# Attention over stacked halves, weight units split by GpSimd, and trimmed ends in a fused attention and feed-forward kernel

## The chip, the cores and the metric

The kernel runs on one core of a Trainium2 chip. The metric is the device time of one execution in microseconds (us). Engines: TensorE (PE, matmuls; PEld its weight loads), VectorE (DVE), ScalarE (ACT), GpSimd (POOL), and SyncE (SP), which only issues DMAs here.

## The reference

128 batches of 64 rows by 1024 columns go through two residual blocks. `itok` names one of 16 conditions for each batch.

```python
def cond(x, weights, condition):            # 64x64 matrix of the batch's condition, mixes the 64 rows
    return jnp.einsum('bct,bcd->bdt', x, weights[condition])

def attn(x, Wqkv, bqkv, Wo, bo):            # one head, d = 256
    q, k, v = split(jnp.einsum('bsc,cf->bsf', x, Wqkv) + bqkv)
    a = softmax(jnp.einsum('bqd,bkd->bqk', q, k) * scale)
    return jnp.einsum('bqd,dc->bqc', jnp.einsum('bqk,bkd->bqd', a, v), Wo) + bo

def cond2(x, ids, weight):                  # 1024x1024 matrix of the batch's condition
    return jnp.einsum('bsi,boi->bso', x, weight[ids])

# ffn: x W^T + b, and a low-rank product whose rank (8, 16, 32, 64) a gate chooses for each row
x = x + attn(cond(x, cond_weights, itok), ...)
x = x + ffn(cond2(x, itok, cond2_weight), ...)
```

## The kernel before

All is computed with numbers kept as two float16 halves, a high and a low one. A product of two such numbers takes three matmuls: high by high, high by low, low by high (the function `three`).

**Phase A (attention).** 64 steps, each with a pair of batches (`a_step(i, q)`; `i` counts 16 bodies of four steps; two pairs make a group of four batches, which lies in a ring of four in SBUF). The row mix and Wqkv are swapped: z = x Wqkv is formed first, then the 64x64 matrix is applied to q, k and, behind the softmax, to v. In a step stand, in this order on TensorE: eight chunks of z for the next pair (`z_part`, L1179, six matmuls each of 128x384), and between them the links of this pair's chain: q/k products (L1214), scores (L1226), transpose of the probabilities (L1231), u = probabilities by mix (L1236), o = z's v part by u (L1244), and four output products of the group before (`out_products`, six matmuls of 128x256). The two batches of a pair share 128 partitions; the mix of a pair is a 128x128 matrix with two 64x64 blocks and zeros beside them (`wcf`, `wch`, `wcl`).

Each link is evicted by ScalarE (high half: `zh`, `qkh`, `pth`, `uh`, `oh`) and then VectorE (low half: `zl`, `qkl`, `ptl`, `ul`, `ol`). Both also split x for the pair after next (`x_hi`, `x_lo`: xs), the next mix (`mix_hi`, `mix_lo`) and add bias and residual for the output products (`out_chunks`, `residual`).

**Weight units.** The 16 matrices of 1024x1024 for phase B are split meanwhile: 64 units of 128x2048 float32 in two stage buffers. For each step ScalarE makes the high half (`unit_hi`, L670) and VectorE the low one (`unit_lo`, L875) in three pieces, and SP stores it to `ws` in DRAM and loads another (`unit_turn`). Four last units (the W of the feed-forward) are split in the first two steps of phase B and stay in SBUF.

**Phase B (feed-forward).** 64 steps with the batches sorted by condition, so that each of the 16 matrices (and one that straddles two streams) is loaded once, in four parts of 1 MB, by GpSimd's DMA queue (`load_condition`, L602). GpSimd works out the order in the first 41 us and then only issues those loads. TensorE runs condition products (`cond_set`, L1284 and L1286), gate and feed-forward (`ffn_main`, L1315 and L1317).

The order on every engine is written out by hand and each instruction waits on semaphores; there is no scheduler. A DMA queue (SP's, GpSimd's) serves its issues in order.

Of the kernel before, what the change touches and what calls it, by code (L numbers as in the profile page):

```python
# [21 lines left out]
ALU = mybir.AluOpType  # L22
# [21 lines left out]
PIECES = ((0, T), (T, T + T // 2), (T + T // 2, 2 * T))  # L44
NPC = len(PIECES)
# [27 lines left out]
def build(nc, NB, x_in, ids_in, wc_in, wqkv_in, wo_in, w2_in, w_in, ag_in, bl_in, bias_in, gb_in, out, x1, ws):  # L73
# [11 lines left out]
    with ctx:  # L85
# [28 lines left out]
        zh_flat = sb("zh", [P, 2 * NQ], F16)  # L114
        zl_flat = sb("zl", [P, 2 * NQ], F16)
        zh = zh_flat[:, :].rearrange("p (r n) -> p r n", r=2)
        zl = zl_flat[:, :].rearrange("p (r n) -> p r n", r=2)
        qkh = sb("qkh", [P, 4, P], F16)
        qkl = sb("qkl", [P, 4, P], F16)
        wcf = sb("wcf", [P, 4, 2 * P], F32)  # L120
        wch = sb("wch", [P, 2, 2 * P], F16)
        wcl = sb("wcl", [P, 2, 2 * P], F16)
        sm = sb("sm", [P, P], F32)
        ex = sb("ex", [P, P], F32)
        pn = sb("pn", [P, P], F32)
        soft = sb("soft", [P, 4], F32)
        pth = sb("pth", [P, P], F16)
        ptl = sb("ptl", [P, P], F16)
# [5 lines left out]
        tt = zh_flat[:, 0:8 * P].bitcast(F32).rearrange("p (r m n) -> p r m n", r=2, m=2)  # L134
        yf = zl_flat[:, 0:8 * P].bitcast(F32).rearrange("p (r m n) -> p r m n", r=2, m=2)
# [67 lines left out]
        bank = [ctx.enter_context(nc.psum_tensor(f"bank{n}", [P, 512], F32)) for n in range(8)]  # L203
        zps = [[bank[0], bank[1]], [bank[2], bank[3]]]
        qkps, chps, wops = bank[4], bank[5], [bank[6], bank[7]]
# [7 lines left out]
        s_wuh, s_wul = sem("unit_piece_hi"), sem("unit_piece_lo")  # L213
# [47 lines left out]
        s_chunk = [sem(f"chunk{n}_loaded") for n in range(NCH)]  # L261

# [53 lines left out]
        def _(sp):  # L316
# [5 lines left out]
            def load_mix(i, q):  # L322

                n = q % 4

                wait(sp, s_wcl, i, 4, q - 3)
                sp.sem_inc(s_turn_sp, 1)
                for b in range(2):
                    e = sp.value_load(idr_i[0:1, bass.ds(8 * i + 2 * q + b, 1)], min_val=0, max_val=NC - 1)
                    dst = wcf[b * S:(b + 1) * S, n, :].rearrange("p (t d) -> p t d", t=2)[:, :, b * S:(b + 1) * S]  # L330
                    src = wc_in[bass.ds(e, 1), :, :, :].rearrange("a c t d -> (a c) t d")
                    sp.dma_start(dst, src).then_inc(s_wc[n], 16)
# [11 lines left out]

            def load_unit(i, q):

                if isinstance(i, int) and 4 * i + q >= UNITS_A:
                    n = 4 * i + q - UNITS_A
                    src = w_in[:, n * UNIT:(n + 1) * UNIT]
                else:  # L350
                    src = w2_in[bass.ds(i, 1), :, q * UNIT:(q + 1) * UNIT].rearrange("a p n -> (a p) n")
                sp.dma_start(stage[:, q % 2, :], src).then_inc(s_unit[q % 2], 16)

            def store_unit(i, q):

                dst = ws[bass.ds(i, 1), :, q, :, :].rearrange("a p h n -> (a p) h n")
                sp.dma_start(dst, split_w[:, q % 2, :, :]).then_inc(s_us[q % 2], 16)

            def unit_turn(i, q, load=True):

                wait(sp, s_wul, i, 4 * NPC, NPC * (q - 1))
                sp.sem_inc(s_turn_sp, 1)
                if q < 2:
                    store_unit(i - 1, q + 2)
                else:
                    store_unit(i, q - 2)
                if load:
                    load_unit(i, q)
# [16 lines left out]
            sp.dma_start(group_cols(0, PT2, PT2), x_in[0, :, PT2:GR]).then_inc(s_x[0], 16)  # L385
# [4 lines left out]
            for n in range(6, K):  # L390
                load_chunk(n)
            load_mix(0, 1)
            for n in range(2):
                sp.sem_inc(s_us[n], 16)
            load_unit(0, 0)
            load_x(0, 1)
            load_unit(0, 1)
# [5 lines left out]
            def body(i, first=False, last=False):  # L403
                for u in range(2):
# [11 lines left out]
                    here = (i, 2) if u == 0 else (i + 1, 0)  # L416
                    late_units = last and u == 1
                    unit_turn(*here, load=not late_units)
# [4 lines left out]
                    unit_turn(here[0], here[1] + 1, load=not late_units)  # L423
                    if late_units:
                        for q in range(2):
                            load_unit(IA, q)
# [36 lines left out]
            for q in range(2, 4):  # L463
                sp.wait_ge(s_wul, NPC * (UNITS_A + q - 1))
                load_unit(IA, q)

# [18 lines left out]
            store_out(IB - 1, 1)  # L485
            for u in range(2):
                sp.wait_ge(s_out[u], 64 * IB)
# [3 lines left out]
        def _(pool):  # L491
# [93 lines left out]
            PACE = 8  # L585

            def load_condition(n):
# [4 lines left out]
                for u in range(2):  # L592
                    pool.wait_ge(s_us[u], 32 * cond + 48)
                    pool.sem_inc(s_turn_pool, 1)
                for t in range(TS):
                    if n == 0:
                        pool.wait_ge(s_z, PACE * (t + 1))
                    else:
# [7 lines left out]
            def first_slots():  # L606
# [4 lines left out]
                pool.wait_ge(s_z, NP)  # L611
# [10 lines left out]
            pool.wait_ge(s_wl, K + 4)  # L622
            pool.wait_ge(s_order, 1)
# [9 lines left out]
        def _(act):  # L633
# [9 lines left out]
            def mix_hi(i, q):  # L643
                wait(act, s_wc[q % 4], i, 32, 32 * (q // 4 + 1))
# [10 lines left out]
            for n in range(K):  # L655
                chunk_hi(n)
                if n == 5:
                    mix_hi(0, 0)
                if n == 6:
                    x_hi(0, 1)  # L660

# [747 lines left out]
```

## Time and profile before

| what | value |
|---|---|
| median of 3 runs | 2286.02 us (2283.11 to 2287.87) |
| the profiled execution's own time | 2283.59 us |
| its span, first to last instruction | 2281.9 us |
| TensorE busy | 2246.7 us, 98% of the span |
| VectorE, ScalarE, GpSimd busy | 1236.8, 953.2, 61.3 us |
| mean granted TensorE clock | 0.999 of full speed |
| DMA engines, slices in phase A | 0.6 to 0.8 busy, 245 to 303 GB/s |
| weight units loaded / stored | 68 / 64 of 1024 KB, 8.8 / 6.9 us from issue to landing (median) |

Busy time says which engine is full; the chain that ended last says what set the end; the timeline of one stretch says how an instruction stands to its neighbours. Times of matmuls overlap, so their cost in a row is read from start to start.

### The profile page before, as it was taken

To read this page: it belongs to the slowest core of one execution; us is meant where nothing else is said; L and a number is where in the kernel's file an instruction comes from. 1 tells how busy PE (TensorE), PEld (TensorE's weight loads), DVE (VectorE), ACT (ScalarE), POOL (GpSimd) and SP (SyncE) were. 2 spreads that over 40 slices of the span, in tenths; PEclk is the share of its full clock that TensorE was granted. 3 is DMA by queue.
4 is the path that set the end of the run, shared out by engine and by line. 5 is a ranking of instruction groups with operands and counts; after the bars stand their busy time and mean duration, and the time that the engine had idled before them with its cause. 6 is when DMAs were issued, how large, how long until landed. Compare 5 with 4: busy or idle time off the path is not lost.

```text
span 2281.9 us, 73807 instructions
## 1 busy us (share of the span) xinstructions
PE 2246.7 (98%) x28506; PEld 1748.9 (77%) x28506; DVE 1236.8 (54%) x3438; ACT 953.2 (42%) x2461; POOL 61.3 (3%) x128
## 2 busy tenths in 40 slices
PE   7999999999999889999999999999999999999998
PEld 4777777777777678887878787878787878787876
DVE  7777777777777754343434444444344444434443
ACT  5776767677767643232322222222222222222221
POOL 4000000000000000000000000000000000000000
PEclk9999999999999999999999999999999999999999
DMA  7668777777677743141214141214225132231303
GB/s 290 249 255 303 272 269 284 272 264 280 245 283 276 271 180 113 44 144 38 93 58 149 39 158 66 76 38 151 74 69 193 39 112 84 103 112 39 131 20 112
DMA packets 108960, 356.46 MB, mean 156 GB/s; under 512 B 27600, under 2 KB 28752, under 8 KB 79184
## 3 DMA queue, kind: packets, MB, share of 16 engines
q1 hardware_dynamic: 98640, 280.89, 34.1%
q0 software_dynamic: 10112, 72.36, 8.5%
q8 instruction: 184, 3.01, 0.5%
q14 instruction: 24, 0.20, 0.0%
HBM read 218.99 MB, written 134.22 MB: 155 GB/s over the span
## 4 chain that ended last, share of the span: by engine, by line
PE 96%; DVE 2%; DMA 1%; ACT 1%; issue 1%; POOL 0%; SPq 0%; DVEq 0%; ACTq 0%; POOLq 0%; PEldq 0%
PE bank L1179 21%; PE bank L1315 19%; PE bank L1284 19%; PE bank L1286 10%; PE bank L1317 10%; PE bank L1136 4%; PE bank L1138 4%; PE bank L1137 4%; PE bank L1297 1%; PE bank L1324 1%; PE bank L1325 1%; PE bank L1299 1%; DMA w<-ws 0%; DVE wf L875 0%; PE bank L1231 0%
## 5 line engine op out<-in xcount | busy, mean ns | idle before, releaser
L1284 PE MATMUL bank<-xs,w 128*128 128x128 f16 x8192 | 625.1, 219 | 3.9 <-DVE xs L882 2.0
L1179 PE MATMUL bank<-w,xs 128*128 128x384 f16 x3072 | 553.2, 327 | 4.4 <-DVE w L895 4.4
L1315 PE MATMUL bank<-y,wf 128*128 128x512 f16 x2048 | 483.8, 379 | 0.8 <-DVE xr L925 0.8
L1284 PEld LDWEIGHTS bank<-xs,w 128*128 128x128 f16 x8192 | 478.2, 98 | 5.8 <-issue 2.4
L763 ACT ACTIVATE zh<-bank 128x256 f32<-128x256 f32 x256 | 97.8, 382 | 777.1 <-PE bank L1286 774.1
L1179 PEld LDWEIGHTS bank<-w,xs 128*128 128x128 f16 x3072 | 290.6, 98 | 165.0 <-issue 2.8
L1286 PE MATMUL bank<-xs,w 128*128 128x64 f16 x8192 | 405.8, 193 | 0.0
L921 DVE SCALAR_TENSOR_TENSOR xr<-bank,xr 128x256 f32 (+1 forms) x256 | 108.6, 424 | 432.7 <-PE bank L1325 387.5
L1315 PEld LDWEIGHTS bank<-y,wf 128*128 128x128 f16 x2048 | 196.9, 98 | 186.6 <-DVE xr L925 1.1
L1286 PEld LDWEIGHTS bank<-xs,w 128*128 128x128 f16 x8192 | 335.9, 98 | 0.0
L1317 PE MATMUL bank<-y,wf 128*128 128x256 f16 x2048 | 265.4, 273 | 0.0
L1317 PEld LDWEIGHTS bank<-y,wf 128*128 128x128 f16 x2048 | 200.5, 98 | 77.7
L925 DVE SCALAR_TENSOR_TENSOR xr<-bank,xr 128x256 f32 (+1 forms) x512 | 216.0, 422 | 48.0 <-PE bank L1138 37.1
L1022 DVE SCALAR_TENSOR_TENSOR zl<-bank,zh 128x256 f32<-128x256 f32 x256 | 107.9, 422 | 244.8 <-ACT zh L763 244.8
L683 ACT ACTIVATE xr<-xr,bias (+1 forms) x512 | 237.7, 502 | 0.0
L765 ACT CAST y<-zl 128x256 f16<-128x256 f32 x256 | 103.7, 405 | 221.6 <-DVE zl L1022 221.6
L882 DVE SCALAR_TENSOR_TENSOR xs<-xr,xs 128x512 f16<-128x512 f16 (+1 forms) x256 | 170.3, 686 | 32.7 <-ACT xs L640 25.3
L1026 DVE TENSOR_TENSOR y<-zl,y 128x256 f16<-128x256 f32 x256 | 108.9, 425 | 120.5 <-ACT y L765 120.5
L875 DVE SCALAR_TENSOR_TENSOR wf<-stage,wf 128x512 f16<-128x512 f32 (+1 forms) x204 | 170.2, 864 | 1.3 <-ACT wf L670 1.3
L670 ACT ACTIVATE wf<-stage 128x512 f16<-128x512 f32 (+1 forms) x204 | 151.1, 784 | 0.0
L640 ACT ACTIVATE xs<-xr 128x512 f16 (+1 forms) x256 | 145.8, 616 | 4.5 <-DMA xr<-x_in 4.5
L1136 PE MATMUL bank<-oh,w 128*128 128x256 f16 x512 | 139.6, 273 | 2.6 <-DVE ol L995 1.4
(158 smaller groups left out, 2083.9 us busy)
## 6 DMA issues: line engine op xcount, KB each, us to landing
stage<-w_in SPq DMA_DIRECT2D x68, 1024.0 KB, 8.8
w<-ws POOLq DMA_DIRECT2D x68, 1024.0 KB, 6.1
ws<-wf SPq DMA_DIRECT2D x64, 1024.0 KB, 6.9
out<-xr SPq DMA_DIRECT2D x128, 256.0 KB, 2.3
xr<-x_in SPq DMA_DIRECT2D x31, 1024.0 KB, 8.0
x<-xr SPq DMA_DIRECT2D x31, 1024.0 KB, 4.4
xr<-x SPq DMA_DIRECT2D x124, 256.0 KB, 3.5
wcf<-wc_in SPq DMA_DIRECT2D x128, 32.0 KB, 4.5
```

The costliest lines, as they stand in the source:

```text
L640: last = nc.scalar.activation(split_view(q, b, 0), batch_view(i, q, b), Copy, scale=SX)
L670: nc.scalar.activation(unit_halves(q, final)[0][:, lo:hi], stage[:, q % 2, lo:hi], Copy, scale=SW).then_inc(s_wuh, 1)
L683: nc.scalar.activation(ring, ring, Iden, bias=bias[:, b0 + m:b0 + m + 1]).then_inc(s_ft, 1)
L875: v.scalar_tensor_tensor(out=low[:, lo:hi], in0=stage[:, q % 2, lo:hi], scalar=SW, in1=high[:, lo:hi], op0=ALU.mult, op1=ALU.subtract).the ...
L882: e = v.scalar_tensor_tensor(out=split_view(q, b, 1), in0=batch_view(i, q, b), scalar=SX, in1=split_view(q, b, 0), op0=ALU.mult, op1=ALU.s ...
L925: v.scalar_tensor_tensor(out=ring, in0=src[m % 2][:, 0:2 * P].rearrange("p (b s) -> p b s", b=4), scalar=scale, in1=ring, op0=ALU.mult, op ...
L1136: mm(dst, ah, bh, start=(k == 0), stop=False)
L1179: e = mm(zps[q % 2][h][:, 0:384], lhs, rhs[:, k, h * 384:(h + 1) * 384], start=(k == 0 and lhs is a and rhs is wq_h), stop=(k == K - 1 and ...
L1284: mm(both, hi[:, k, c], x_k, start=(k == 0), stop=False)
L1286: e = mm(y_m[:, at], lo[:, k, c], x_pair[:, k, at], start=False, stop=(k == K - 1))
L1315: mm(fps[m % 2][:, :], wf_h[:, k, c], yhl[:, u, k, :], start=(k == 0), stop=False)
L1317: mm(fps[m % 2][:, 0:2 * P], wf_l[:, k, c], yh[:, u, k, :], start=False, stop=False)
```

## The change

z is evicted batch by batch into `zs`: for each batch one half-of-partitions block holds the 64 rows' high half and the other the same rows' low half. A product with it then contracts 128 partitions that are the two halves of one batch, and needs two matmuls of 64 columns for each batch (by the high and the low half of the mix, which is loaded twice, above and below) instead of three of 128 for the pair. So it is for the q/k products and o, and, with the transposed probabilities stacked in `pt`, for u. The q blocks go to one bank of PSUM, the k blocks to z's own. The step's order changes on all engines: three z chunks stand ahead of the q/k products, the third output product stands ahead of the transpose and the fourth ahead of u, x is split ahead of the q/k eviction. The mix is loaded in four DMAs for a pair instead of two.

`unit_hi`, `unit_lo`, `load_unit`, `store_unit` and `unit_turn` leave ScalarE, VectorE and SP. GpSimd does all 68 units in a loop of its own with no wait for the steps, the four last ones included, and asks for phase B's first condition only behind them (it was asked for in the course of phase A). At the start the second half of the first x group is loaded behind the Wqkv chunks; at the end the last group's output is stored in three pieces.

```diff
+            def split_unit(i, q, final=False):
+                high, low = unit_halves(q, q if final else None)
+                wait(pool, s_unit[q % 2], i, 32, 16 * (q // 2) + 16)
...
+                elif not final:
+                    wait(pool, s_us[q % 2], i, 32, 16 * (q // 2))
...
+                halves = [slice(n, n + T) for n in range(0, UNIT, T)]
+                for c in halves:
+                    st = stage[:, q % 2, c]
+                    pool.tensor_scalar(high[:, c], st, SW, 1.0, ALU.mult, ALU.mult).then_inc(s_uhi, 1)
+                    pool.tensor_scalar(st, st, SW, 1.0, ALU.mult, ALU.mult).then_inc(s_uhi, 1)
+                for h, c in enumerate(halves):
+                    wait(pool, s_uhi, i, 16, 4 * q + 2 * h + 2)
+                    pool.tensor_tensor(low[:, c], stage[:, q % 2, c], high[:, c], ALU.subtract).then_inc(s_ulo, 1)
+            def units(i, last=False):
+                for q in range(4):
+                    split_unit(i, q)
+                    wait(pool, s_ulo, i, 8, 2 * q + 2)
+                    dst = ws[bass.ds(i, 1), :, q, :, :].rearrange("a p h n -> (a p) h n")
+                    pool.dma_start(dst, split_w[:, q % 2, :, :]).then_inc(s_us[q % 2], 16)
+                    load_unit(i if q < 2 else i + 1, (q + 2) % 4)
...
+            units(NC - 1, last=True)
+            for q in range(4):
+                split_unit(NC, q, final=True)
...
             load_condition(0)
@@ ScalarE, z_hi @@
-                for h in range(2):
-                    e = nc.scalar.activation(zh[:, q % 2, h * 384:(h + 1) * 384], zps[q % 2][h][:, 0:384], Copy,
-                                             scale=SZ / (SX * SW))
+                for b in range(2):
+                    at = slice(b * S, (b + 1) * S)
+                    nc.scalar.activation(zs_two[at, q % 2, b, :, :], zboth[q % 2][at, :, :], Copy,
+                                         scale=SZ / (SX * SW)).then_inc(s_zh, 1)
@@ VectorE, a_step @@
-                    unit_lo(i, q, (0, 1))
...
+                if ahead and not first:
+                    x_lo(i, q + 2, 0)
...
-                if not end:
-                    unit_lo(i, q, (2,))
@@ TensorE, a_step @@
-                zz(0, 1)
+                zz(0, 1, 2)
...
-                for c in range(4):
-                    d = slice(c * P, (c + 1) * P)
-                    e = three(qkps[:, d], [(zh[:, r, d], zl[:, r, d], wch[:, r, 0:P], wcl[:, r, 0:P])])
+                for b in range(2):
...
+                    for c in range(4):
+                        dst, z_c = qk_block(r, c)[:, at], zs[:, r, b, c * P:(c + 1) * P]
+                        mm(dst, z_c, wch[:, r, mix], start=True, stop=False)
+                        e = mm(dst, z_c, wcl[:, r, mix], start=False, stop=True)
...
-                three(chps[:, 0:P], [(wch[:, r, P:2 * P], wcl[:, r, P:2 * P], pth[:, :], ptl[:, :])]).then_inc(s_u, 1)
+                for b in range(2):
...
+                        e = mm(chps[:, at], twice, pt[:, at], start=(half == 0), stop=(half == 1))
```

GpSimd, in the loop over the units (phase A), in the changed kernel; its lines are those of the changed file (`stage` is the float32 unit, `wf` the split one; L593 is `load_unit`, L612 and L613 the one-input passes, L616 the two-input one, L623 the store, L69 and ISA registers and waits):

```order
L593 DMA stage<-w_in 128x2048
L612 TENSOR_SCALAR wf<-stage 128x1024
L613 TENSOR_SCALAR stage<-stage 128x1024
L612 TENSOR_SCALAR wf<-stage 128x1024
L613 TENSOR_SCALAR stage<-stage 128x1024
L69 REGISTER_ALU
L616 TENSOR_TENSOR wf<-stage,wf 128x1024
L69 REGISTER_ALU
L616 TENSOR_TENSOR wf<-stage,wf 128x1024
L69 REGISTER_ALU
L623 ISA
L623 DMA ws<-wf 128x4096
```

Before, GpSimd had none of these; behind the order of the batches stood the loads of phase B (`L602 DMA w<-ws 128x4096`) at once, and the store and load of a unit stood on SP.

VectorE, in the loop over the bodies of phase A, the front of a step, before (L875 `unit_lo`, L954 qkl, L889 `mix_lo`, L925 `residual`, L966 the scores' mask and maximum `sm`, L970 and L972 the softmax):

```order
L875 SCALAR_TENSOR_TENSOR wf<-stage,wf 128x1024
L70 REGISTER_ALU
L875 SCALAR_TENSOR_TENSOR wf<-stage,wf 128x512
L954 SCALAR_TENSOR_TENSOR qkl<-bank,biasq,qkh 128x128 x4
L889 SCALAR_TENSOR_TENSOR wcl<-wcf,wch 128x256
L70 REGISTER_ALU
L925 ISA
L925 SCALAR_TENSOR_TENSOR xr<-bank,xr 128x4x64
L966 ISA sm,soft<-bank,mask 128x128
L966 ISA soft 128x1
L970 RECIPROCAL soft<-soft 128x1
L972 TENSOR_SCALAR pn<-ex,soft 128x128
```

The same place in the changed kernel (L866 `x_lo`, L939 qkl, L873 `mix_lo`, L907 `residual`, L949 `sm`, L953 the softmax; `zbanks` are z's banks, where the k blocks lie now):

```order
L866 ISA
L866 SCALAR_TENSOR_TENSOR xs<-xr,xs 128x8x64
L939 SCALAR_TENSOR_TENSOR qkl<-bank,biasq,qkh 128x128 x2
L939 SCALAR_TENSOR_TENSOR qkl<-zbanks,biasq,qkh 128x128 x2
L873 SCALAR_TENSOR_TENSOR wcl<-wcf,wch 128x384
L69 REGISTER_ALU
L907 ISA
L907 SCALAR_TENSOR_TENSOR xr<-bank,xr 128x4x64
L949 ISA sm,soft<-bank,mask 128x128
L949 ISA soft 128x1
L953 RECIPROCAL soft<-soft 128x1
```

Ahead of qkl the unit pieces went and half of an x split came; the mix has 384 columns instead of 256.

VectorE, the back of a step, before (L979 ptl, L882 `x_lo`, L986 ul, L932 zl, L995 ol):

```order
L979 TENSOR_TENSOR ptl<-bank,pth 128x128
L882 ISA
L882 SCALAR_TENSOR_TENSOR xs<-xr,xs 128x8x64
L70 REGISTER_ALU
L925 ISA
L925 SCALAR_TENSOR_TENSOR xr<-bank,xr 128x4x64
L986 SCALAR_TENSOR_TENSOR ul<-bank,uh 128x128
L932 SCALAR_TENSOR_TENSOR zl<-bank,zh 128x384 x2
```

The same place in the changed kernel (L964 the low half of `pt`, L969 ul, L914 the low half of z):

```order
L964 TENSOR_TENSOR pt<-bank,pt 64x128
L69 REGISTER_ALU
L907 ISA
L907 SCALAR_TENSOR_TENSOR xr<-bank,xr 128x4x64
L866 ISA
L866 SCALAR_TENSOR_TENSOR xs<-xr,xs 128x8x64
L969 SCALAR_TENSOR_TENSOR ul<-bank,uh 128x128
L69 REGISTER_ALU
L907 ISA
L907 SCALAR_TENSOR_TENSOR xr<-bank,xr 128x4x64
L69 REGISTER_ALU
L914 SCALAR_TENSOR_TENSOR zs<-zbanks,zs 64x768
```

The second half of the x split now stands directly ahead of ul, and both residual additions stand ahead of z's low halves, which are two instructions of 64 partitions by 768 columns with a wait each.

## Rows read from the trace of the kernel before

**Rows 1.** The page, part 4, the chain that ended last by engine.
```profile
PE 96%; DVE 2%; DMA 1%; ACT 1%; issue 1%; POOL 0%; SPq 0%; DVEq 0%; ACTq 0%; POOLq 0%; PEldq 0%
```

**Rows 2.** Busy time of each engine in a stretch of phase A.
```profile
160.00:500.00 340.00, 340.00 (x2826) 243.36 (x2825) 262.09 (x681) 239.46 (x622) 1.59 (x3) 1.00 0.75 276
```

**Rows 3.** Timeline of TensorE in one step of phase A: start, us, instruction.
```profile
398.05 0.22 PE L1136 MATMUL bank<-wch,zh 128*128 128x128 f16 x1
...
398.72 2.11 PE L1179 MATMUL bank<-w,xs 128*128 128x384 f16 x12
...
406.00 0.22 PE L1136 MATMUL bank<-pth,wch 128*128 128x128 f16 x1
...
406.17 1.14 PE L1179 MATMUL bank<-w,xs 128*128 128x384 f16 x6
...
407.80 0.22 PE L1136 MATMUL bank<-uh,zh 128*128 128x128 f16 x1
...
408.14 2.11 PE L1179 MATMUL bank<-w,xs 128*128 128x384 f16 x12
410.09 0.22 PE L1136 MATMUL bank<-wch,zh 128*128 128x128 f16 x1
```

**Rows 4.** The chain in order of time, in phase B.
```profile
810.76 0.23 PE bank L1286 x8
810.99 0.45 PE bank L1284 x8
```

**Rows 5.** Timeline of VectorE in the same step.
```profile
401.14 0.41 DVE L889 SCALAR_TENSOR_TENSOR wcl<-wcf,wch 128x256 f16<-128x256 f32 x1
...
404.05 0.69 DVE L882 SCALAR_TENSOR_TENSOR xs<-xr,xs 128x512 f16<-128x512 f16 x1
...
406.72 0.28 DVE L986 SCALAR_TENSOR_TENSOR ul<-bank,uh 128x128 f16<-128x128 f32 x1
408.25 1.02 DVE L932 SCALAR_TENSOR_TENSOR zl<-bank,zh 128x384 f16<-128x384 f32 x2 [1.25 <-ACT zh L689]
```

**Rows 6.** Timeline of ScalarE in the same step.
```profile
406.37 0.28 ACT L728 ACTIVATE uh<-bank 128x128 f16<-128x128 f32 x1 [1.12 <-PE bank L1138]
407.35 0.87 ACT L689 ACTIVATE zh<-bank 128x384 f16<-128x384 f32 x2 [0.70 <-PE bank L1179]
```

**Rows 7.** Timeline of GpSimd, the first 41 us and at 780.
```profile
3.12 0.29 POOL L517 CAST ident<-ident 128x128 f16<-128x128 f32 x1
...
11.59 0.82 POOL L532 TENSOR_SCALAR per_c<-per_c 16x1 f32<-16x1 f32 x1
...
25.18 1.01 POOL L552 TENSOR_TENSOR wf<-wf 16x16 f32<-16x16 f32 x4
...
28.52 2.63 POOL L552 TENSOR_TENSOR wf<-wf 16x16 f32<-16x16 f32 x4
...
31.52 0.45 POOL L554 TENSOR_SCALAR wf<-wf,per_c 16x17 f32<-16x17 f32 x1
32.06 0.58 POOL L555 TENSOR_SCALAR wf<-wf,per_c 16x64 f32<-16x64 f32 x1
...
37.52 0.19 POOL L566 CAST order<-wf 1x17 int32<-1x17 f32 x1
...
40.77 0.22 POOL L576 TENSOR_SCALAR order<-late 1x1 int32<-1x1 f32 x1
...
780.04 2.36 POOL L619 DMA_DIRECT2D xr<-x  x4 [383.55 <-PE bank L1179]
```

**Rows 8.** The page, part 6, DMA issues: size, median us to landing.
```profile
w<-ws POOLq DMA_DIRECT2D x68, 1024.0 KB, 6.1
```

**Rows 9.** Timeline of TensorE, the first product of phase B.
```profile
800.00 0.62 PE L1284 MATMUL bank<-xs,w 128*128 128x128 f16 x8 [1.87 <-DVE xs L882]
```

**Rows 10.** Timeline of VectorE at the start.
```profile
10.50 3.56 DVE L895 SCALAR_TENSOR_TENSOR w<-w 128x768 f16<-128x768 f32 x4
```

**Rows 11.** Timeline at the end of the span, SP's issues.
```profile
2277.35 1.93 SPq L453 DMA_DIRECT2D out<-xr  x4
```

More of the change, by code:

```diff
@@ L624, in _ @@
+            units(0)
+            with pool.Fori(1, NC - 1) as i:
+                units(i)
+            units(NC - 1, last=True)
+            for q in range(4):
+                split_unit(NC, q, final=True)
+                if q < 2:
+                    wait(pool, s_ulo, NC, 8, 2 * q + 2)
+                    load_unit(NC, q + 2)
             load_condition(0)
@@ L792, in b_step @@
                     gate_exp(pi, pu)
-                if first and q == 0:
-                    for n in range(2):
-                        act.wait_ge(s_us[n], 16 + 16 * UNITS_A // 2)
                 y_set(i, q, 1)
@@ L904, in _ @@
                     link(dve_copy(2, UPTO, trps[0:NC, 0:1]))
-                if n == 5:
-                    mix_lo(0, 0)
-                if n == 6:
-                    for b in range(2):
-                        x_lo(0, 1, b)
+            mix_lo(0, 0)
+            for b in range(2):
+                x_lo(0, 1, b)
             def residual(i, u, ms, phase_b=False):
@@ L949, in a_step @@
                     oo(0)
[L950 to L952 removed]
+                elif isinstance(i, int) and i == 0 and q >= 2:
+                    chunk_lo(K + 2 + q)
+                ahead = not (last and q >= 2)
+                first = isinstance(i, int) and i == 0 and q == 0
+                if ahead and not first:
+                    x_lo(i, q + 2, 0)
                 for c in range(4):
[L954 removed]
+                    wait(dve, s_qkh, i, 8, 2 * q + c // 2 + 1)
+                    e = v.scalar_tensor_tensor(out=qkl[:, c, :], in0=qk_block(q % 2, c),
                                                scalar=biasq[:, c:c + 1], in1=qkh[:, c, :], op0=ALU.add,
@@ L971, in a_step @@
                 wait(dve, s_r, i, 4, q + 1)
-                v.tensor_scalar(pn[:, :], ex[:, :], soft[:, 2:3], SP, ALU.mult, ALU.mult).then_inc(s_p, 1)
-                if not end:
-                    unit_lo(i, q, (2,))
-                if not (last and q >= 2):
+                for b in range(2):
+                    at = slice(b * S, (b + 1) * S)
+                    block = ex[at, at].rearrange("p (a n) -> p a n", a=1).to_broadcast([S, 2, S])
+                    e = v.tensor_scalar(pn[at, :, :], block, soft[at, 2:3], SP, ALU.mult, ALU.mult)
+                e.then_inc(s_p, 1)
+                if ahead and first:
                     x_lo(i, q + 2, 0)
```

265 lines of the change are left out of this document (111 added, 154 removed).

## The prediction

> **What bounds the kernel now.** I read the chain that ended last first: TensorE is 96% of it [rows 1]. Then the busy time by stretch: in the attention stage (160 to 500 us shown) TensorE is busy for all 340 us, VectorE for 262 and ScalarE for 239, and GpSimd for 1.6 [rows 2]. So a saving counts there only if it shortens TensorE's own row of matmuls, and other engines matter where they start to make it wait. Then TensorE's timeline over one step (one pair of batches): from the first q/k product at 398.05 to the next one's at 410.09, 12.04 us with no gap [rows 3]. 64 such steps make the stage. The feed-forward stage begins at 800.00 [rows 9] and runs to the end; the diff leaves its steps alone but for the four last weight units in its first steps.
>
> **TensorE's part of the change.** The step's q/k products were 12 matmuls of 128 columns and took 398.05 to 398.72, 0.67 us; u took 406.00 to 406.17, 0.17; o 407.80 to 408.14, 0.34 [rows 3]. They become 16, 4 and 8 matmuls of 64 columns. What such a matmul costs when each has its own 128-column weights, the feed-forward stage shows: eight in 0.23 us against eight of 128 columns in 0.45 [rows 4], 0.029 each. So 0.46, 0.12 and 0.23: 0.81 against 1.18, **0.37 us a step**, 24 us in 64 steps. z, scores, transpose and out products stay as they are. New step: 11.67 us.
>
> **Is there cover for the longer chains in it?** z is now evicted by batch: 64 partitions by 768 columns, twice. Partitions run side by side, so each of these does the column work of the old pair, which took 0.87 us on ScalarE and 1.02 on VectorE [rows 5, 6]; these are upper bounds. The chain behind the last z product: z ended at 406.17 + 6 x 0.1625 (twelve took 1.95 [rows 3]) = 407.15 and ScalarE began at 407.35 [rows 6], 0.20 later; then 0.87, and two low halves of at most 1.02: 3.1 us. The cover on TensorE is o (0.23) and three z chunks instead of two (2.92): 3.15. It fits, barely. The link from u to o: 0.20, uh 0.28, ul 0.28 with some 0.1 of wakes [rows 5, 6], 0.86 against one z chunk, 0.975. Between the scores and the transpose there is a z chunk and two out products, 2.3 us, for sm, exponent, reciprocal and two halves of pn. So without a disturbance no wait appears, but margins that were near 0.8 us (zl done at 409.27, wanted at 410.09 [rows 3, 5]) are 0.1.
>
> **VectorE and ScalarE.** Both lose the unit pieces, some 2.5 us a step, and VectorE pays back about 1 us for the longer z halves. That makes nothing faster by itself, but it takes two pieces out of the way of qkl.
>
> **GpSimd's part decides the sign.** It now does for each of 64 + 4 units four one-input passes and two two-input passes of 128x1024, a store and a load. The trace has no such operation; it is bounded so.
> One-input pass: a cast of 128 columns took 0.29 us and one of 17 took 0.19 [rows 7], 0.9 ns a column: 1.08 us for 1024. Dearest: tensor_scalar with a compare, 0.58 at 64 columns and 0.45 at 17 [rows 7], 2.8 ns a column: 3.0 us. I take 1.08, since scaling by constants compares nothing.
> Two-input pass: four small ones take 1.01 us when alone [rows 7], so 0.2 fixed; for the columns I take two reads at 0.9 ns: 2.0 us. Below that, one read: 1.1; above, 3.0.
> Issues: four DMAs in 2.36 us [rows 7], 0.59 each, 1.2 a unit; waits between dependent operations some 0.2.
> Together 4 x 1.08 + 2 x 2.0 + 1.4 = **9.7 us a unit**.
> Then VectorE gets in its way. The same four small operations took 2.63 us at 28.52, while VectorE ran instructions with two operands in SBUF, instead of 1.01 [rows 7]; so did the one of 16 elements at 11.59, 0.82. Such instructions remain in each step: two x_lo of 0.69 and a mix_lo that grows from 0.41 to about 0.55 [rows 5], 1.9 us. Per unit that costs at most 1.9 x 9.7 / 11.67 x 0.86 (the share of a unit in which GpSimd reads SBUF) = 1.4, at least nothing. Middle: 0.7, so 10.4 us.
> The deadline: units start when the order is written, 41.0 [rows 7], plus a load of 6.1 [rows 8], at 47. Phase B's first weights are asked for only behind the last unit on GpSimd's queue and need 6.1 to land. TensorE gets there at 800 - 24 - 3 = 773, so GpSimd must be done at 766. 719 us for 68 units, of which four have no store: **10.6 us a unit is the point from which GpSimd decides**. At 10.4 it ends at 47 + 64 x 10.4 + 4 x 9.8 = 752, in time. Each 0.1 over 10.6 costs 6.8 us.
> VectorE may also have to wait. VectorE's four pieces at 10.50 took 3.56 us, evenly 0.87 apart, with GpSimd's small operations between them [rows 7, 10]: no delay seen, but those held nothing for long. Lower bound 0; upper, an x_lo or mix_lo that stands for the rest of a pass (0.6 us on the mean, up to 2.0): against margins of 0.4 to 0.8 ahead of qkl, sm and ul I work out 0.7 us a step at most. I take 0.12, 8 us in all, for the thinnest link (u to o).
> The Trainium skill speaks against this change here: in "SBUF — State Buffer", section "Who interferes with whom", the pair of ports is an exclusive lock held for a whole instruction by whoever came first, with the other one fully blocked. The trace agrees as to GpSimd (2.63 instead of 1.01) and shows nothing as to VectorE; by the rule the upper ends hold, 1.4 a unit and 0.7 a step. "GPSIMD Engine Reference", section "Elementwise — side-by-side cycle accounting", has 4497 ns for a two-input add of 2048 columns; no run here shows it, and with half of that a unit would be 0.5 us longer and late by itself once the lock is added.
>
> **DMA.** Units leave SP's queue for GpSimd's: 2 MB per 10.4 us. What runs behind each unit's turn on SP (x loads, x1 stores, mixes) no longer waits for it. Mix issues double; they are loaded two pairs ahead. A unit's load has a whole unit's time, 10.4, to land where 1 MB took 6.1 [rows 8]. I cost it at nothing; with the store ahead of it in the same queue it may come to 10 and then hold GpSimd, which belongs to the first rival.
>
> **Ends.** At the start 0.5 MB of x moves behind the last weight chunks and the mix and second x splits go behind the chunks: about 1 us; the first steps have no out products and lose the unit pieces: 1 to 2. At the seam the last four units' pieces leave the first feed-forward steps: 3 us of the small waits there, such as the 1.87 at 800.00 [rows 9]. At the end four issues took 1.93 us [rows 11]; the last two chunks now go out in the same number of issues with a quarter of the bytes: 0.5. Together 6, with 2 and 10 as its ends.
>
> **Sum**, against the profiled execution's own 2283.6 us (2.4 below the median of the runs, 2286.0): 2283.6 - 24 - 6 + 8 = 2261.6, **2262**.
>
> **Rivals.**
> GpSimd is late (this one ends on the other side). Place: the first feed-forward products, waiting for weights that are loaded behind the 68th unit. It decides from 10.6 us a unit. At 9.7 + 1.4 = 11.1 the start comes 34 us late: 2254 + 34 = 2288, no gain. With two-input passes 0.3 longer, 11.7: 2254 + 75 = 2329. At 3.0 a one-input pass it would be beyond 2700. For it: the pass times come from tiny operations. Against it: four of six passes have one input, the cheapest kind seen. Chance 0.28, of which 0.02 ends faster and 0.06 within the bound named below.
> VectorE stands behind GpSimd's passes and TensorE behind qkl, sm and ul: 0.7 us x 64 = 45, 2254 + 45 = 2299. It decides from 0.45 us a step. Chance 0.12, of which 0.02 within the bound.
> The 64-column matmuls don't gain, because each loads its own 128 columns of weights: 2278. [rows 4] speak against it. Chance 0.03.
> Forecast: chance 0.57, 2243 to 2275.
>
> **How the numbers follow.** About 0.2% (4.6 us) is what a measurement of this kernel can tell from no change: 2281.4 to 2290.6 is "same". Faster: forecast 0.57, the 64-column case 0.03, and 0.02 of the first rival, 0.62. Same: 0.06 and 0.02 of the two rivals, 0.08. Slower: the rest, 0.30. The forecast's own range is 2243 to 2275; to hold 8 in 10 it has to reach into the late GpSimd, to 2325, while 1 in 20 lies below 2243.
>
> **What would show it.** Right: steps of 11.7 us on TensorE, q/k products 0.46 long, no wait there in the stretch from 160 to 500; GpSimd's one-input passes near 1.1, two-input near 2.0, units 10.4 apart, the last ending before 766; the feed-forward stage starting near 770. Wrong: TensorE idle at the seam until a weight load lands (first rival); rows of qkl, sm or ul that TensorE waits for in every step, with x_lo longer than 0.69 (second).

## The result and the profile after

2599.56 us (median of 4 runs, 2579.43 to 2605.08) against 2285.11 before: a ratio of 1.136, 95% interval 1.129 to 1.143, **slower** by 314 us where 24 less were forecast. The profiled execution took 2579.43 us, its span 2577.4. One of psum_operand_2's six runs below (2394.98 us) fell in a slower state of the core and is left out of its figures.

The page of the changed kernel shows where: TensorE's busy tenths and the granted clock in 40 slices of the span (part 2), and the chain that ended last (part 4).
```profile
PE   6466778677479999999999999999999999999999
PEclk9688888888689999999999999999999999999999
PE 84%; issue 9%; DVE 5%; ACT 1%; SPq 0%; DVEq 0%; DMA 0%; ACTq 0%
```
TensorE's gaps end with slice 12, near 770 us; in the chain TensorE has 84% where it had 96% [rows 1]. The same by stretch, columns as in [rows 2]: the stretch and its length, busy us and number of instructions of TensorE, its weight loads, VectorE, ScalarE and GpSimd, then the granted clock, the DMA engines' busy share and GB/s.
```profile
160.00:500.00 340.00, 236.71 (x1831) 153.28 (x1829) 299.17 (x381) 127.08 (x324) 316.70 (x263) 0.85 0.74 265
500.00:760.00 260.00, 170.07 (x1272) 107.13 (x1270) 232.53 (x261) 88.65 (x226) 228.25 (x190) 0.81 0.70 251
820.00:1080.00 260.00, 258.93 (x2365) 183.16 (x2362) 189.51 (x489) 163.29 (x417) 2.16 (x4) 1.00 0.30 103
```
While GpSimd works (317 of 340 us) TensorE is busy for 237 us and did 1831 recorded matmuls instead of 2826 [rows 2]; behind 820, with GpSimd still, it is full again at a clock of 1.00. A granted clock between its two levels, 1.00 (2.4 GHz) and 0.50 (1.2 GHz), is a mean over the stretch. The feed-forward stage starts at 1102.73 instead of 800.00 [rows 9] and is 7 us shorter than before (1474.7 against 1481.9), so the whole loss lies in the attention stage.

Where GpSimd is quiet the step is near the forecast. TensorE's timeline there, one step, to set beside [rows 3]:
```profile
911.16 0.19 PE L1197 MATMUL bank<-wch,zs 128*128 128x64 f16 x1
...
911.63 2.11 PE L1154 MATMUL zbanks<-w,xs 128*128 128x384 f16 x12
...
919.69 0.19 PE L1234 MATMUL bank<-uh,zs 128*128 128x64 f16 x1
...
919.92 3.09 PE L1154 MATMUL zbanks<-w,xs 128*128 128x384 f16 x18
...
922.85 0.19 PE L1197 MATMUL bank<-wch,zs 128*128 128x64 f16 x1
```
q/k take 0.47 us, o 0.23, the step 11.69. So it is in three of four steps there (11.68); every fourth takes 11.92, the mean is 11.74. GpSimd's timeline, one unit and the last pass of the last one:
```profile
56.90 1.06 POOL L612 TENSOR_SCALAR wf<-stage 128x1024 f16<-128x1024 f32 x1
...
60.94 4.19 POOL L616 TENSOR_TENSOR wf<-stage,wf 128x1024 f16<-128x1024 f32 x2
...
66.60 1.06 POOL L612 TENSOR_SCALAR wf<-stage 128x1024 f16<-128x1024 f32 x1
...
742.15 4.19 POOL L616 TENSOR_TENSOR wf<-stage,wf 128x1024 f16<-128x1024 f32 x2
```
The unit shown takes 9.7 us, the 68 of them 10.3 on the mean, and the last ends at 746.3: in time. So who is late? What TensorE waited for from 45 to 760 us (total, times, longest), and VectorE's two longest groups from 160 to 500 (count, busy us, mean ns):
```profile
PE bank L1111 <- DVE qkl L939: 113.6, 22, 12.4
PE bank L1234 <- DVE ul L969: 62.3, 20, 7.4
PE bank L1215 <- DVE pn L958: 49.4, 18, 8.3
PE bank L1111 <- DVE xr L907: 16.3, 3, 6.7
```
```profile
L866 DVE SCALAR_TENSOR_TENSOR xs<-xr,xs 128x512 f16<-128x512 f16 x35 | 157.2, 4491 | 1.1
L958 DVE TENSOR_SCALAR pn<-ex,soft 64x128 f32<-64x128 f32 x34 | 32.9, 967 | 0.8
```
x_lo (L866), 0.69 us before [rows 5], has a mean of 4.49. From 45 to 760 us 31 of 67 x_lo took over 5 us, and so did 3 mix_lo and 3 pn; one x_lo, at 732.56, stood 14.33 us, through the rest of one unit and all of the next, which follows it with no store between. One place shows it on three engines, VectorE, GpSimd and TensorE (in brackets the idle time before the row and who ended it):
```profile
303.15 8.89 DVE L866 SCALAR_TENSOR_TENSOR xs<-xr,xs 128x512 f16<-128x512 f16 x1
311.96 0.28 DVE L969 SCALAR_TENSOR_TENSOR ul<-bank,uh 128x128 f16<-128x128 f32 x1
```
```profile
303.25 1.06 POOL L612 TENSOR_SCALAR wf<-stage 128x1024 f16<-128x1024 f32 x1
...
307.29 4.20 POOL L616 TENSOR_TENSOR wf<-stage,wf 128x1024 f16<-128x1024 f32 x2
```
```profile
312.30 0.23 PE L1234 MATMUL bank<-uh,zs 128*128 128x64 f16 x1 [7.41 <-DVE ul L969]
```
GpSimd's six passes follow each other from 303.25 to 311.49. x_lo began 0.10 us ahead of the first and ended 0.55 behind the last, somewhat less than its own 0.69. ul stands behind it on VectorE's queue, and TensorE behind ul. Then it repeats:
```profile
178.57 8.71 DVE L866 SCALAR_TENSOR_TENSOR xs<-xr,xs 128x512 f16<-128x512 f16 x1
...
199.25 8.75 DVE L866 SCALAR_TENSOR_TENSOR xs<-xr,xs 128x512 f16<-128x512 f16 x1
...
219.77 8.96 DVE L866 SCALAR_TENSOR_TENSOR xs<-xr,xs 128x512 f16<-128x512 f16 x1
```
20.6 us lie between them: 11.7 of step and 9 of standing, or two units of 10.3. The end of a unit releases VectorE, and so sets the place of the next x_lo against the next unit but one.

The sum: from 45 to 760 us TensorE waited for 242.6 us. It also ran at 0.78 to 0.85 of its clock, from 1.00 before: 472 busy us for 3563 recorded matmuls, which at the 339.49 us for 3102 of a full stretch (thin_paced_mix_first, below) are 390 us of work; 82 lost. Together some 325, of which the shorter step gives some 20 back: the 303 by which the feed-forward stage starts later.

### The profile page after: what moved, and what is told of

It is laid out like the page before. It is cut to its first block, busy times and chain, and to the rows that moved or that the text cites. A ratio compares the mean times of both kernels' runs of the same rounds, so it can differ in the third digit from the quotient of the medians.

```text
span 2577.4 us, 75193 instructions
## 1 busy us (share of the span) xinstructions
PE 2307.8 (90%) x28954; PEld 1753.4 (68%) x28954; DVE 1534.6 (60%) x3298; ACT 881.4 (34%) x2257; POOL 710.3 (28%) x668
## 4 chain that ended last, share of the span: by engine, by line
PE 84%; issue 9%; DVE 5%; ACT 1%; SPq 0%; DVEq 0%; DMA 0%; ACTq 0%
PE zbanks L1154 18%; PE zbanks L1273 18%; PE bank L1304 17%; PE zbanks L1275 9%; PE bank L1306 9%; PE bank L1111 2%; PE bank L1113 2%; PE bank L1112 2%; DVE xs L866 2%; PE bank L1286 1%; PE bank L1314 1%; PE bank L1313 1%; DVE qkl L939 1%; DVE pn L958 1%; PE bank L1288 1%
## 5 line engine op out<-in xcount | busy, mean ns | idle before, releaser
L1273 PE MATMUL zbanks<-xs,w 128*128 128x128 f16 x8192 | 625.1, 219 | 1.9 <-DVE xs L866 1.9
L1154 PE MATMUL zbanks<-w,xs 128*128 128x384 f16 x3072 | 602.0, 347 | 3.4 <-DVE w L879 2.1
L1273 PEld LDWEIGHTS zbanks<-xs,w 128*128 128x128 f16 x8192 | 478.2, 98 | 3.7 <-issue 2.1
L866 DVE SCALAR_TENSOR_TENSOR xs<-xr,xs 128x512 f16<-128x512 f16 (+1 forms) x256 | 432.9, 1712 | 31.4 <-ACT xs L654 26.2
L1154 PEld LDWEIGHTS zbanks<-w,xs 128*128 128x128 f16 x3072 | 302.8, 104 | 191.5 <-issue 46.1
L1275 PE MATMUL zbanks<-xs,w 128*128 128x64 f16 x8192 | 405.9, 193 | 0.0
L1275 PEld LDWEIGHTS zbanks<-xs,w 128*128 128x128 f16 x8192 | 335.9, 98 | 0.0
L616 POOL TENSOR_TENSOR wf<-stage,wf 128x1024 f16<-128x1024 f32 x136 | 295.0, 2184 | 0.0
L1003 DVE SCALAR_TENSOR_TENSOR zs<-zbanks,zs 128x256 f32<-128x256 f32 x256 | 108.2, 423 | 252.2 <-ACT zs L765 252.2
L907 DVE SCALAR_TENSOR_TENSOR xr<-bank,xr 128x256 f32 (+1 forms) x512 | 216.4, 423 | 42.3 <-PE bank L1113 28.7
L1007 DVE TENSOR_TENSOR y<-zs,y 128x256 f16<-128x256 f32 x256 | 109.0, 426 | 120.7 <-ACT y L767 120.7
L612 POOL TENSOR_SCALAR wf<-stage 128x1024 f16<-128x1024 f32 x136 | 147.0, 1081 | 10.1 <-DMA ws<-wf 4.3
```

The lines of the kernel that those rows point to most:

```text
L612: pool.tensor_scalar(high[:, c], st, SW, 1.0, ALU.mult, ALU.mult).then_inc(s_uhi, 1)
L616: pool.tensor_tensor(low[:, c], stage[:, q % 2, c], high[:, c], ALU.subtract).then_inc(s_ulo, 1)
L866: e = v.scalar_tensor_tensor(out=split_view(q, b, 1), in0=batch_view(i, q, b), scalar=SX, in1=split_view(q, b, 0), op0=ALU.mult, op1=ALU.s ...
L907: v.scalar_tensor_tensor(out=ring, in0=src[m % 2][:, 0:2 * P].rearrange("p (b s) -> p b s", b=4), scalar=scale, in1=ring, op0=ALU.mult, op ...
L1007: v.tensor_tensor(yl[:, q // 2, 2 * t:2 * t + 2, c], yf[:, t % 2, :, :], yh[:, q // 2, 2 * t:2 * t + 2, c], ALU.subtract).then_inc(s_yl, 1)
L1154: e = mm(zps[q % 2][h][:, 0:hi - lo], lhs, rhs[:, k, lo:hi], start=(k == 0 and lhs is a and rhs is wq_h), stop=(k == K - 1 and lhs is b))
```

## The experiments

The theory: GpSimd's back-to-back passes hold VectorE's instructions with two operands in SBUF for the whole run of passes. Rivals: the new order has too little slack; the transfers on GpSimd's queue disturb; the lower clock is the cause. Each run is compared with runs of the kernel before on the same chip (medians 2285 to 2286).

**Which part of the change?** units_back puts the units back on ScalarE, VectorE and SyncE and keeps the rest of the change.
```diff
-            units(0)                          # GpSimd
...
+                    unit_hi(i, q, (0,))       # ScalarE, and (1,), (2,) later in the step
...
+                    unit_lo(i, q, (0,))       # VectorE, likewise
```


> Keeps the stacked halves, the new order of the step and the trimmed ends, and puts the weight units back on ScalarE, VectorE and SyncE as before. Theory 'GpSimd's passes hold VectorE': nothing of the loss is in the step itself, so the time comes back to 2255 to 2300 us (TensorE's step is 11.69 us where GpSimd is quiet, but VectorE then has about 8.7 + 2.4 us of work in it, so some of the gain of 0.37 us a step may be lost again), the x_lo instructions of VectorE have a mean near 0.69 us, and TensorE runs at a granted clock of 1.00 from 160 to 500 us. Rival 'the new order is too tight': VectorE and TensorE wait for each other as in the changed kernel, 2500 us or more.

2307.77, ratio 1.0095 (1.0078 to 1.0112), 8 us above the range expected: no long x_lo (0.69 at most), clock 1.00. units_alone is the other half, the kernel before with its units on GpSimd.
```diff
-                    unit_hi(i, q, (0, 1))     # and all other unit pieces on ScalarE, VectorE, SyncE
...
+            with pool.Fori(1, NC - 1) as i:
+                units(i)
```


> The kernel before with one part of the change alone: all weight units on GpSimd, loads and stores on its queue; the step's order, the products of whole pairs and both ends stay as before. Theory 'GpSimd's passes hold VectorE, whatever the step': VectorE's x_lo stands for 7 to 9 us here too, and the time is 2450 to 2650 us. Rival 'the new order has too little slack between VectorE and TensorE, the old one has enough': 2280 to 2350 us.

2577.18, ratio 1.128 (1.125 to 1.131): the whole loss, without the new order. It is not x_lo that stands there, as was expected (3 of 68 took over 3 us), but pn and mix_lo (VectorE's lines, 160 to 500 us):
```profile
L940 DVE TENSOR_SCALAR pn<-ex,soft 128x128 f32<-128x128 f32 x17 | 73.6, 4328 | 0.6
L859 DVE SCALAR_TENSOR_TENSOR wcl<-wcf,wch 128x256 f16<-128x256 f32 x17 | 68.2, 4011 | 0.0
```
pn reads `ex` and one column of `soft`, so an instruction with one full operand in SBUF can stand too. From 45 to 760 us 35 of these three kinds took over 3 us, against 37 in the changed kernel: about one a step in either, whichever comes at that place. So the rival of the order falls. Yet units_back shows that the new order is no gain either with the units on VectorE: 12.38 us a step on the mean, in which TensorE waits 0.29 for a residual and, in many, up to 0.4 behind a late qkl.

**Is it the run of passes?** drain makes GpSimd wait for the end of each pass.
```diff
                     pool.tensor_scalar(high[:, c], st, SW, 1.0, ALU.mult, ALU.mult).then_inc(s_uhi, 1)
+                    wait(pool, s_uhi, i, 16, 4 * q + 2 * h + 1)
...
                     pool.tensor_scalar(st, st, SW, 1.0, ALU.mult, ALU.mult).then_inc(s_uhi, 1)
+                    wait(pool, s_uhi, i, 16, 4 * q + 2 * h + 2)
...                                           # and one behind each two-input pass
```


> The changed kernel, with GpSimd waiting after each of a unit's six passes until that pass has completed, so that its passes are no longer back to back. Theory 'the passes hold VectorE for as long as they follow each other': VectorE gets in between two passes, an x_lo stands for the rest of one pass (1.05 or 2.1 us) and not for 7 to 9 us; 2300 to 2400 us, and units some 0.5 us longer. Rival 'GpSimd's transfers or its load as such disturb': nothing changes, 2580 to 2600 us.

2363.46, ratio 1.034 (1.032 to 1.036). Some 0.19 us between passes is enough: VectorE's x_lo, and the stretch:
```profile
L871 DVE SCALAR_TENSOR_TENSOR xs<-xr,xs 128x512 f16<-128x512 f16 x57 | 74.4, 1306 | 2.5
```
```profile
160.00:500.00 340.00, 335.65 (x3005) 230.33 (x3004) 284.79 (x619) 208.91 (x533) 289.99 (x225) 1.00 0.76 276
```
None of 117 x_lo is longer than 2.52 us, the clock is 1.00 and the step 12.1, with transfers at much the same rate. It is the gap and not another place: 51 of these x_lo came from 0.03 us before to 0.22 after the start of a unit's first pass, where in the changed kernel nearly all stand to the unit's end, and got in within 1.64 us. One of them on VectorE, and GpSimd's first two passes:
```profile
165.65 1.47 DVE L871 SCALAR_TENSOR_TENSOR xs<-xr,xs 128x512 f16<-128x512 f16 x1
```
```profile
165.51 1.06 POOL L612 TENSOR_SCALAR wf<-stage 128x1024 f16<-128x1024 f32 x1
166.85 1.16 POOL L615 TENSOR_SCALAR stage<-stage 128x1024 f32<-128x1024 f32 x1 [0.29 <-POOL wf L612]
```
The price is that a unit now takes 12.0 us on the mean, and the feed-forward stage waits for the last, the forecast's first rival:
```profile
883.93 1.03 PE L1278 MATMUL zbanks<-xs,w 128*128 128x128 f16 x8 [72.55 <-DMA w<-ws]
```

**The passes taken away.** thin_passes leaves loads, stores and the number of passes, and makes them short: 16 columns of 1024, so that most of a unit stays unsplit.
```diff
-                halves = [slice(n, n + T) for n in range(0, UNIT, T)]
+                halves = [slice(n, n + (T if final else 16)) for n in range(0, UNIT, T)]
```


> The changed kernel, in which each of GpSimd's passes over a unit covers 16 columns of each half instead of 1024 (phase B's condition weights are therefore mostly left unsplit, zero); loads, stores, waits and the number of passes stay. Theory 'the passes hold VectorE': what is left of a pass is some 0.1 us, so x_lo stands nowhere and the time is 2250 to 2275 us, with a step of 11.7 us from 160 to 500 us. Rival 'the transfers on GpSimd's queue, or the order of the step': 2500 us or more, as the transfers are the same.

2447.73, a miss of mine: unheld, the units came as fast as the queues gave, at 362 GB/s from 160 to 500 us instead of 265, and ScalarE waited for mixing weights (12 times, 136.6 us from 45 to 760). thin_paced ties a unit to a step:
```diff
+                if not final and not (isinstance(i, int) and i == 0):
+                    wait(pool, s_t, i, 4, q - 3)
```


> Thin passes as in the run before it (16 columns of each half; phase B's condition weights mostly left at zero), but a unit starts only when the attention step four before its own has passed its transposes, so that loads and stores come one unit a step as in the changed kernel and not as fast as the queues take them. Theory 'the passes hold VectorE': nothing holds it now, the step is 11.7 us from 160 to 500 us and the time 2255 to 2290 us. Rival 'the transfers on GpSimd's queue disturb at any rate': 2400 us or more, as in the unpaced run (2447.73).

2476.17, no better and a miss again, though no x_lo is over 0.69. What ScalarE waits for, 160 to 760 us:
```profile
ACT wch L665 <- DMA wcf<-wc_in: 119.0, 20, 7.4
```
A **second cause**. On SyncE the two loads of mixing weights are queued behind the load of x, which waits until the store of x ahead of it has landed (9.6 us at the median here, 4.3 in drain). thin_paced_mix_first moves them ahead of it:
```diff
                 for u in range(2):
+                    for j in range(2):        # load_mix(i, q + 2), moved up from below load_x
                     if not last:
                         wait(sp, s_st[u], i, 16, 0)
                         load_x(i + 1, u)
```


> thin_paced (16 columns a pass, condition weights mostly left at zero), with the loads of mixing weights ahead of the waiting load of x on SyncE. Theory 'thin_paced lost its time (2476.17 us) to mixing weights that land late behind a store and a load of x on SyncE': ScalarE's waits for them, 119.0 us between 160 and 760 us there, go, and the time is 2270 to 2310 us. Rival 'GpSimd's transfers fill the queues and anything behind them is late': the waits stay, 2400 us or more.

2295.65, ratio 1.005 (1.003 to 1.006): those waits are gone, and TensorE is full at 11.7 us a step:
```profile
160.00:500.00 340.00, 339.49 (x3102) 240.77 (x3100) 249.00 (x637) 216.28 (x551) 77.83 (x232) 1.00 0.79 285
```
What is left lies at the ends: against the kernel before, 11 us up to the eighth step's transpose and 22 behind the 61st, where the last four units run at full width and unpaced and one x_lo stands for 7.71 us. mix_first_alone asks whether this repair (the same edit on SyncE) helps the changed kernel:

> The changed kernel with the one repair on SyncE alone: the loads of mixing weights ahead of the load of x that waits. VectorE's operands and GpSimd stay. Theory 'the late mixing weights are a second cause, hidden as long as VectorE stands': nothing to gain yet, 2550 to 2610 us, x_lo as before at a mean of several us. Rival 'late transfers are the larger part of the loss': 2450 us or less.

2582.95, ratio 1.130: no. ScalarE has no such wait there, nor in the changed kernel; TensorE's step is so long that the weights are in time. x_lo had a mean of 2.20 us from 160 to 500; from 45 to 760 us 13 x_lo, 13 pn and 11 mix_lo took over 3 us, again 37.

**Which pass holds?** In thin_paced, one kind of pass gets its full width again, the two-input ones in thin_one_input, the one-input ones in thin_two_input.
```diff
-                one, two = ([slice(n, n + (T if final else w)) for n in range(0, UNIT, T)] for w in (16, 16))
+                one, two = ([slice(n, n + (T if final else w)) for n in range(0, UNIT, T)] for w in (16, T))
```

> As thin_paced, but with the two two-input passes of a unit at full width (4.19 us in a row); the four one-input passes stay at 16 columns, so the condition weights are left wrong. Theory 'a run of passes holds VectorE until it ends, whatever the passes': an x_lo stands up to 4.2 us, the time is 2300 to 2420 us. Variant 'the one-input passes alone hold it, since a VectorE instruction was seen to get in between the two two-input passes': x_lo stands for the rest of one pass, at most 2.1 us, and the time is 2260 to 2320 us.

> As thin_paced, but with the four one-input passes at full width (4 x 1.05 us in a row) and the two two-input passes at 16 columns, so the condition weights are left mostly without their low part. Theory 'a run of passes holds VectorE until it ends, whatever the passes': an x_lo stands up to 4.2 us, 2300 to 2420 us, much as with the two-input passes alone. Variant 'the one-input passes alone hold it': the time is longer than with the two-input passes alone, 2320 to 2450 us, and x_lo instructions of 4 us appear here and not there.

2383.30 and 2308.90, at 13.0 and 11.7 us a step. In both the x_lo arrives during a pass and gets in at its end. thin_one_input, VectorE and GpSimd:
```profile
406.01 2.55 DVE L871 SCALAR_TENSOR_TENSOR xs<-xr,xs 128x512 f16<-128x512 f16 x1
```
```profile
405.90 4.65 POOL L619 TENSOR_TENSOR wf<-stage,wf 128x1024 f16<-128x1024 f32 x2
```
It stands for one of the two passes, and the two together take 0.46 longer than the 4.19 of the changed kernel. My theory of the whole run, whatever the passes, falls in this form. Its variant forecast x_lo of 4 us with the one-input passes alone, and none came (1.35 at most). That doesn't refute it: the paced x_lo come 0.78 us into the first pass there, a place at which they get in with all passes at full width too, as the next run shows.

**What decides, then?** full_paced has `for w in (T, T)` in that line: all passes at full width, one unit a step at a fixed place behind the first body (four steps), whose units still run free.

> The changed kernel with all passes at full width, in which a unit starts when the attention step four before its own has passed its transposes: one unit a step, always at the same place of the step, and the full result. Theory 'an x_lo that is there when a unit's first pass starts stands to the unit's end, one that comes during a pass often gets in at that pass's end, and the free-running units fall in step with the x_lo they hold up': no x_lo stands 8 us any more, at most 2.6 us in most steps, 2330 to 2420 us with some 20 us of it at the end of the stage, where the last four units run behind each other. Rival 'what counts is only how long GpSimd's passes take in a step': 8.4 us of passes a step as before, x_lo stands 7 to 9 us, 2500 us or more.

2366.23, ratio 1.036 (1.034 to 1.037). Passes follow each other without a gap, and yet:
```profile
L871 DVE SCALAR_TENSOR_TENSOR xs<-xr,xs 128x512 f16<-128x512 f16 x55 | 51.7, 940 | 2.4
```
From 160 to 745 us the paced x_lo come 0.8 us into the first pass (47 of them) or during the two-input ones (47), and all get in. Ahead of that, with units still free, two came 0.05 and 0.43 us behind a unit's start and stood to its end (8.73 and 8.35 us). In the changed kernel 59 x_lo met a unit between 45 and 745 us. Of 21 that came from 0.25 us before to 0.52 after the start of its first pass, 20 stood to its end. Of 13 that came later in the one-input passes, 10 stood. Of 22 that came in the two-input passes none stood for longer than one pass. Three came 0.38 to 0.46 before the unit, and one of them stood. So the place in the unit matters, the free-running units keep VectorE at the worst one, and the fixed place avoids it.

The place alone doesn't decide: in mix_first_alone only 5 of 9 in the same stretch from 0.26 before to 0.52 after stood, of four that came 0.04 to 0.05 behind the start two stood and two got in, and one that came 0.81 behind it stood to the end. What tells them apart isn't settled. Of the time, most was lost before pacing began: against the kernel before, full_paced is 60 us behind at the eighth step's transpose, loses 10 more up to the 61st (12.23 us a step) and 21 at the seam.

**Operands in PSUM.** psum_operand_2 takes away the sharing itself: ScalarE copies the high halves of x and of the mixing weights into a PSUM bank that is free at that time, and writes the exponentials, pn's operand, to PSUM. x_lo's part:
```diff
+                nc.scalar.copy(xps[b].rearrange("p (k s) -> p k s", k=K),
+                               xs_words[:, q % 2, :, b * S // 2:(b + 1) * S // 2]).then_inc(s_xp, 1)
                 e = v.scalar_tensor_tensor(out=split_view(q, b, 1), in0=batch_view(i, q, b), scalar=SX,
-                                           in1=split_view(q, b, 0), op0=ALU.mult, op1=ALU.subtract)
+                                           in1=xps[b].bitcast(F16).rearrange("p (k s) -> p k s", k=K),
```


> The changed kernel, in which ScalarE copies the high halves of x and of the mixing weights once more, into a PSUM bank that TensorE is not using at that time, and writes the exponentials to PSUM: x_lo, mix_lo and pn on VectorE then read one operand from PSUM and one from SBUF. GpSimd's passes, loads and stores stay word for word. ScalarE has three copies more a step, some 1.0 us. Theory 'VectorE stands where both its operands are in SBUF': x_lo stays below 1 us on the mean while GpSimd's passes run, TensorE keeps a granted clock of 1.00 from 160 to 500 us, and the time is 2250 to 2300 us. Rival 'any VectorE instruction that touches SBUF stands while GpSimd's passes follow each other': x_lo still has a mean of several us and the time is 2500 us or more.

2323.44 (median of five runs, 2319.37 to 2351.35), ratio 1.019 (1.015 to 1.023): the mechanism as expected, the time not. VectorE's x_lo, 160 to 500 us, beside unchanged passes of GpSimd:
```profile
L898 DVE SCALAR_TENSOR_TENSOR xs<-xr,bank 128x512 f16<-128x512 f16 x53 | 36.2, 683 | 18.3 <-ACT bank L666 18.3
```
None of 107 is over 0.69. What remained is the second cause, and a pn that comes late (57 waits of TensorE, 31.2 us), as mix_lo with its copy stands ahead of it. SyncE's queue: store, then the load that waits for it, then the mixing weights.
```profile
325.37 0.41 SPq L349 DMA_DIRECT2D x<-xr  x1
330.15 0.35 SPq L326 DMA_DIRECT2D xr<-x_in  x1
332.86 7.71 SPq L338 DMA_DIRECT2D wcf<-wc_in  x8
```
psum_mix_first adds the repair on SyncE and puts mix_lo, with its copy, behind pn.
```diff
                 oo(1 if end else 0)
-                if not end:
-                    mix_lo_psum(i, q + 1)
...
                 e.then_inc(s_p, 1)
+                if not end:
+                    mix_lo_psum(i, q + 1)
```

> psum_operand_2 with two repairs: on SyncE the two loads of mixing weights stand ahead of the load of x that waits until a store of x has landed, and mix_lo (with ScalarE's copy for it) stands behind pn instead of ahead of the mask of the scores. GpSimd as in the changed kernel. Theory 'what psum_operand_2 still loses is the late mixing weights (13 waits of ScalarE, 33.5 us, between 160 and 760 us) and pn coming 0.55 us late in each step (28.9 us)': both waits go, the step comes to 11.7 to 11.9 us and the time to 2265 to 2295 us. Rival 'transfers bunch up and something else of them is late': ScalarE or TensorE wait for another load, 2310 us or more.

**2270.78, ratio 0.9934 (0.9920 to 0.9947): 14 us less than the kernel before**, a small gain but clear of the noise, with GpSimd doing all units. Its stretch and its first feed-forward product:
```profile
160.00:500.00 340.00, 339.34 (x3090) 238.64 (x3089) 245.90 (x636) 241.43 (x638) 316.45 (x268) 1.00 0.88 313
```
```profile
796.13 0.62 PE L1312 MATMUL zbanks<-xs,w 128*128 128x128 f16 x8 [2.07 <-DVE xs L889]
```

## Why the prediction was wrong, point by point

- **TensorE, −0.37 us a step**: right in kind, somewhat large. Three of four steps take 11.68 against 12.04, every fourth 11.92: 0.30 on the mean, 19 us in 64 steps instead of 24.
- **Cover for the longer chains**: right. With nothing in VectorE's way (thin_paced_mix_first) TensorE is busy 339.49 of 340 us; two z halves take 1.94 us on VectorE, within the 2.04 allowed.
- **GpSimd, 9.7 us a unit, in time at 752**: right. One-input passes 1.05 (1.08 taken), two-input 2.10 (2.0). It ended at 746.3, at 10.3 a unit against the 10.4 taken with the lock. The Trainium skill's "GPSIMD Engine Reference", section "Elementwise — side-by-side cycle accounting", is near the trace here: half of its 4497 ns, as an estimate, is 2.25 us.
- **VectorE behind GpSimd, 0.12 us a step taken, 0.7 at most**: the step that failed. "the rest of a pass (0.6 us on the mean, up to 2.0)" assumed that a waiting x_lo gets in at the end of a pass, and that it comes at a random moment of it. No row bore either out; [rows 7, 10] hold only small operations with gaps. Measured: nearly every x_lo that comes as a unit starts stands for all six passes, 8.2 us, and the two loops keep each other in that position, so 31 of 67 x_lo, 3 mix_lo and 3 pn stood for over 5 us, about one a step, and a locked step cost 9 us more, not 0.7. The rival of this name was the right mechanism, priced at 45 us for 64 steps where the stage grew by 303. An upper bound from my own numbers was at hand: six passes, 8.3 us, once a step, 530 us.
- **The Trainium skill's rule** ("SBUF — State Buffer", section "Who interferes with whom": the lock is held for a whole instruction by the first comer) was the warning. thin_one_input and full_paced agree with it, the changed kernel's rows go beyond it: x_lo stood through six instructions. The same section says that a VectorE instruction with at most one input in SBUF doesn't contend, outside the 2-port perf modes; psum_operand_2 agrees as to x_lo (0.683 against 4.491 us).
- **DMA, at nothing**: wrong, but hidden behind the larger loss. With nothing in VectorE's way the late mixing weights alone cost 180 us (thin_paced, 2476.17 against 2295.65). With operands in PSUM they and a late pn cost 53 (2323.44 against 2270.78, in one edit for both).
- **The lower clock**: a consequence of TensorE's waits, as far as the runs show. From 160 to 500 us it was 1.00 in drain, full_paced and psum_mix_first, with the same passes and transfers, and 0.92 in thin_paced, where TensorE waited for another reason; in thin_one_input, with short waits (309.91 of 340 us busy), it stayed at 1.00.
- **Ends, −6**: 7.2 us came behind the seam, in the changed kernel and in psum_mix_first alike. Of the 27 us before it psum_mix_first got 4. It gained 14 between the eighth and the 61st step's transpose (11.77 us a step); up to there it had lost 6, with one wait of 5.90 for qkl at 68.77, and behind it lost 4 more, which wasn't pursued.

## What to carry to other kernels

Work that is moved to GpSimd as a run of passes over SBUF must be priced by the run, not by the pass, for each VectorE instruction with two operands in SBUF that can come at its start; and two loops that hold each other up don't meet at random, they can lock. Before such a move, give VectorE one operand in PSUM, or leave 0.2 us between the passes. When a repair brings less than it should, look for a second wait that the first one had hidden, here a load queued behind another load's wait.

## What the runs showed of the hardware

An x_lo that had begun 0.26 us ahead of GpSimd's first pass, and needs 0.69 alone, still stood to the end of the run (9.04 us at 385.50, the pass at 385.76): being first by a little didn't help it. Sometimes it did: the x_lo at 416.54, 0.02 us ahead of a unit, took 0.69, and GpSimd's first pass took 1.57 instead of 1.06. A gap of some 0.19 us between passes helped every time (117 x_lo in drain, 2.52 us at most). The same x_lo with one operand in PSUM took 0.68 us on the mean and 0.69 at most beside the same passes.
